# A macaron block on one core: the order of VectorE and ScalarE inside an attention step

## The chip, the cores and the metric

The kernel is written for one NeuronCore of a Trainium2 chip and runs on that core alone. The metric is device time in microseconds (us) of one execution, lower is better. TensorE, VectorE, ScalarE, GpSimd and SyncE are meant by these names; in rows of the profile they are PE (PEld for its weight loads), DVE, ACT, POOL and SP.

## What is computed

The input is x, 8 batches of 512 tokens of 128 values. Three layers follow, each on the layer-normed x and added to it: a mixture of experts (8 experts, top 2, hidden size 512) with weight one half, causal attention with 16 heads of 64, and the same mixture of experts again. The change touches the attention only:

```python
q = jnp.einsum('ahe,bce->bach', W_Q, x)
k = jnp.einsum('ahe,bce->bach', W_K, x)
v = jnp.einsum('ahe,bce->bach', W_V, x)
scores = jnp.einsum('bach,baCh->bacC', k, q)
masked = jnp.where(causal, scores, jnp.float32(-MASK_VAL))
attn = jax.nn.softmax(masked / np.float32(np.sqrt(D_HEAD)), axis=-1)
z = jnp.einsum('bacC,baCh->bach', attn, v)
out = jnp.einsum('aeh,bach->bce', W_O, z)
```

The rows of the scores belong to k, and the softmax runs over the tokens of q. Everything is fp32.

## The kernel before

Each engine has a program of its own, written out by hand, and semaphores join them. Nothing is scheduled by a planner: the order on an engine is the order of the calls in its function.

The attention is a loop of 64 steps (STEPS), eight for each batch; step i is one pair of heads of one batch, and its place in the batch is s. The 512 tokens of k are four tiles t of 128; causality makes tile t only (t + 1) x 128 columns wide, so a step has maxima and exponentials of 512, 384, 256 and 128 columns, two of each (heads h = 0, 1). A product of fp32 precision is made of high and low parts (split_matmul): ScalarE copies k and q from their banks rounded to k_hi and q_hi (take_k, take_q), VectorE subtracts these from the banks and gets k_lo and q_lo (split_k, split_q, "the low parts"), and the scores are three matmuls of them.

In a step i the engines do, in this order:

- TensorE: scores of tiles 3, 2, 1, 0 of step i; attend(i - 2), whose second half reads the late squares, which come by DMA; project_k and project_q of step i + 1 (they wait for the maxima of tile 2, whose banks they use); transposes(i - 1) of the early squares into the banks of tile 3; project_out(i - 2); project_v. The scores of step i + 1 wait for both low parts (qk_lo_ready) and for ScalarE's copies of the transposed squares (pt_act).
- VectorE: the maxima of tiles 3 (then the reciprocal of the last step's sums), 2, 1 and 0, which also add the mask and write the scores to SBUF; divide_by_sums(i - 2), which needs attend; turn_long, which turns the six late squares of each head by 32 x 32 blocks in two instructions; four pieces of side work; the low parts of step i + 1; up to seven more pieces of side work. Side work (go_on, finish) is layer norm and routing for other batches, spread over the steps by hand. In the fifth step of a batch (s = 4) it ends with split_for_attention, which makes xn_lo of the next batch.
- ScalarE: exps of tiles 3, 2 and 1; take_k and take_q of step i + 1; transposed(i - 1), two copies; exps of tile 0; take_v. At s = 4 and s = 5 (route_step) a further copy stands ahead of take_v.
- SyncE: store_sums and load_long of step i - 1, spread_sums, then store_long of step i: four stores of 192 KB of the turned squares to DRAM once turn_long has signalled, from where load_long fetches all of them in one DMA of 768 KB, back in the right place for attend. SyncE takes these one after another; load_long waits for the four stores (turned_stored) and for attend two steps back, whose late half reads the buffer it fills.

max_ready is what VectorE's maxima signal: S_USES = 3 times a step, after both heads of tile 3, after both of tile 2, after tiles 1 and 0.

## Time and profile before

| | before |
|---|---|
| time, median of 3 runs | 951.3 us (951.26 to 952.12) |
| the profiled execution: its own time, and its span | 942.84 us, 940.7 us |
| TensorE busy | 859.9 us, 91% of the span |
| VectorE busy | 812.2 us, 86% |
| ScalarE busy | 674.7 us, 72% |
| GpSimd busy | 279.9 us, 30% |
| mean granted clock of TensorE | 0.992 |

The attention steps lie between about 182 and 788 us of the span, the experts ahead of them and behind them. The profiled execution is one execution, and not one of the three that were timed. A row of the order in time has the start in us, the duration in us, the engine, the line of kernel.py, the operation, what it writes and reads and how many instructions it groups; in brackets how long the engine was idle just before it, and who ended that.

### The profile page before, as it was taken

The page shows a single profiled execution, that of the slowest core. Times are in us where ns is not written, and L with a number is a line of the kernel's source. Part 1 is how long each engine was busy: PE and PEld are TensorE (multiplying, and loading weights), DVE is VectorE, ACT ScalarE, POOL GpSimd, SP SyncE. Part 2 cuts the span into 40 slices and gives each one's busy share as a digit, 9 for nine tenths or more (in the row PEclk, how much of TensorE's full clock was granted, in tenths as well). Part 3 has the DMA queues.
Part 4 walks back from the last instruction along what each step waited for, and adds up shares of the span by engine and source line. Part 5 has one row for each costly group of instructions (what it writes and reads, how often), then busy time and mean ns, then how long its engine had stood idle before and what let it go on. Part 6 is the DMA issues. An engine that isn't in the chain of part 4 may idle for free.

```text
span 940.7 us, 24331 instructions
## 1 busy us (share of the span) xinstructions
PE 859.9 (91%) x7378; PEld 737.2 (78%) x7378; DVE 812.2 (86%) x3083; ACT 674.7 (72%) x1977; POOL 279.9 (30%) x328
## 2 busy tenths in 40 slices
PE   7999999978999998998998998999899888999994
PEld 6889998866777777776777776777687776999994
DVE  7878888789899899899999999989989996786666
ACT  3787667577777867785877786777686775787881
POOL 5777103241111021312321312310200102567551
PEclk9999999999999999999999999999999999999998
DMA  9677556177788688777687778676766785557657
GB/s 248 217 221 245 183 156 199 46 210 175 230 227 215 206 239 215 221 209 206 187 242 182 233 204 225 190 235 199 214 195 209 185 231 159 168 159 212 218 158 225
DMA packets 141296, 190.40 MB, mean 202 GB/s; under 512 B 35328, under 2 KB 108832, under 8 KB 141168
## 3 DMA queue, kind: packets, MB, share of 16 engines
q1 hardware_dynamic: 128256, 168.56, 61.1%
q0 software_dynamic: 8352, 18.17, 7.8%
q10 hardware_dynamic: 4560, 2.12, 0.8%
q8 instruction: 61, 1.00, 0.5%
q14 instruction: 67, 0.55, 0.2%
HBM read 114.04 MB, written 74.74 MB: 201 GB/s over the span
## 4 chain that ended last, share of the span: by engine, by line
PE 36%; DVE 25%; issue 5%; DMA 4%; SPq 2%; ACT 0%; POOL 0%; POOLq 0%; DVEq 0%; ACTq 0%
PE psum L2552 8%; PE psum L2502 7%; DVE arena L1975 6%; PE psum L2387 5%; DVE arena L1960 4%; PE psum L2338 3%; PE psum L2340 3%; PE psum L2339 3%; DVE arena L1990 3%; DVE q_lo L1947 2%; PE psum L2585 2%; PE psum L2541 2%; DVE k_lo L1951 1%; DMA turned_dram<-arena 1%; DVE bn L1243 1%
## 5 line engine op out<-in xcount | busy, mean ns | idle before, releaser
L1130 ACT ACTIVATE arena<-arena,neg_max 128x512 f32<-128x512 f32 (+3 forms) x512 | 281.5, 553 | 145.0 <-DVE neg_max L1960 142.7
L1960 DVE CUSTOM_DVE_ANT_0 arena<-psum,causal 128x512 f32<-128x512 f32 (+3 forms) x512 | 217.1, 480 | 29.0 <-PE psum L2502 28.5
L1074 ACT ACTIVATE arena<-psum,b_t 128x256 f32<-128x256 f32 (+1 forms) x336 | 120.8, 442 | 40.6 <-PE psum L2340 31.4
L876 POOL DMA_INDIRECT arena<-y_tiles,y_at x64 | 61.0, 953 | 277.6 <-PE psum L2502 194.3
L2387 PE MATMUL psum<-w_sb,arena 128*128 x1136 | 141.5, 276 | 0.2 <-ACT arena L1074 0.2
L2387 PEld LDWEIGHTS psum<-w_sb,arena 128*128 128x128 f32 x1136 | 134.9, 193 | 0.4 <-issue 0.4
L857 POOL DMA_INDIRECT x_slots<-xr,slot x64 | 61.9, 968 | 237.9 <-PE psum L2502 190.1
L2502 PE MATMUL psum<-q_hi,k_lo 64*128 64x512 f32 (+3 forms) x512 | 87.0, 332 | 42.0 <-DVE q_lo L1947 41.8
L1975 DVE STREAM_TRANSPOSE arena<-arena 128x768 f32<-128x768 f32 x126 | 115.7, 960 | 4.7 <-DMA turned_dram<-arena 2.8
L2502 PEld LDWEIGHTS psum<-q_hi,k_lo 64*128 64x128 f32 x512 | 49.0, 185 | 70.6 <-DVE q_lo L1947 65.0
L1130 ACT ACTIVATION_READ_ACCUMULATOR arena<-arena,neg_max 128x1 f32 x512 | 97.4, 190 | 0.0
L2552 PE MATMUL psum<-y_all,arena 128*64 128x128 f32 x1008 | 93.0, 327 | 2.3 <-DMA y_all<-turned_dram 2.3
L2502 PE MATMUL psum<-q_lo,k_hi 64*128 64x512 f32 (+3 forms) x512 | 84.1, 321 | 0.0
L2502 PE MATMUL psum<-q_hi,k_hi 64*128 64x512 f32 (+3 forms) x512 | 83.8, 319 | 0.0
L2552 PEld LDWEIGHTS psum<-y_all,arena 128*64 128x64 f32 x1008 | 66.2, 138 | 20.8 <-DMA y_all<-turned_dram 2.5
L885 POOL DMA_INDIRECT y_rows<-y_all,y_tok x69 | 67.4, 977 | 41.2 <-DVE y_all L1830 26.3
L1990 DVE TENSOR_TENSOR arena<-psum,arena 128x512 f32<-128x512 f32 x64 | 69.3, 1083 | 7.9 <-PE psum L2552 6.1
L857 POOL DMA_INDIRECT x_slots<-arena,slot x64 | 64.1, 1001 | 28.7 <-issue 16.2
L2552 PE MATMUL psum<-arena 128*64 128x128 f32 (+1 forms) x532 | 71.6, 392 | 0.2 <-ACT arena L1140 0.2
L1140 ACT ACTIVATE arena<-psum 128x512 f32<-128x512 f32 x129 | 68.6, 584 | 0.3 <-PE psum L2541 0.3
L2541 PE MATMUL psum<-ident,arena 128*128 128x128 f32 x524 | 67.8, 272 | 0.3 <-ACT arena L1140 0.3
L2585 PE MATMUL psum<-wo_t,arena 128*128 128x128 f32 x512 | 67.7, 275 | 0.2 <-DVE arena L1990 0.2
(361 smaller groups left out, 1989.9 us busy)
## 6 DMA issues: line engine op xcount, KB each, us to landing
turned_dram<-arena SPq DMA_DIRECT2D x252, 192.0 KB
y_all<-turned_dram SPq DMA_DIRECT2D x63, 768.0 KB, 5.2
arena<-inv_dram SPq DMA_DIRECT2D x128, 128.0 KB
w_raw<-in_L_ffn_W_dram SPq DMA_DIRECT2D x60, 256.0 KB
xg<-x_slots SPq DMA_DIRECT2D x43, 144.0 KB
arena<-in_L_ffn_W_dram SPq DMA_DIRECT2D x24, 256.0 KB
arena<-y_rows SPq DMA_DIRECT2D x16, 256.0 KB, 4.8
y_tiles<-y_all SPq DMA_DIRECT2D x27, 128.0 KB, 1.9
```

The lines of the kernel that those rows point to most:

```text
L857: pool.indirect_dma_start(out=x_slots[f][:, :], out_offset=bass.IndirectOffsetOnAxis(ap=slot[f][:, k, at_tile:at_tile + 1], axis=0), in_=r ...
L1074: ins = act.activation(h_t[side(f, n)][:, k, 0:rows], H_BANKS[side(f, n)][k // 2][:, k % 2 * rows:(k % 2 + 1) * rows], ACT.Relu, bias=b1_t ...
L1130: ins = act.activation(prob_tile(i, h, t), prob_tile(i, h, t), ACT.Exp, scale=-1.0, bias=neg_max[i % 2][:, h, t:t + 1], accum_out=row_sum[ ...
L1140: act.activation(four_turned(g), turned_bank(i, g), ACT.Copy).then_inc(pt_act, 1)
L1960: ins = dve.tensor_tensor_reduce(out=prob_tile(i, h, t), in0=score_tile(t, h), in1=causal[:, SEQ - (t + 1) * P:SEQ], scale=-1.0, scalar=-2 ...
L1975: ins = dve.transpose(long_block(h), long_probs(i, h).rearrange("p (n j s) -> p n j s", n=len(LATE_SQUARES), s=BLOCK))
L1990: dve.tensor_tensor(z_sb.rearrange("p (t q) -> p t q", t=QT), RING_C.rearrange("p (t q) -> p t q", t=QT), inv_bc[i % 2].rearrange("p q t - ...
L2387: ins = pe.matmul(Y_BANKS[side(f, n)][:, r * D:(r + 1) * D], h_t[side(f, n)][:, k, r * P:(r + 1) * P], w2_sb[:, bass.ds(e * (CHUNKS * D) + ...
L2502: ins = pe.matmul(score_tile(t, h), k[m, tile], q[m, 0:(t + 1) * P], start=(n == 0), stop=(n == 2))
L2541: ins = pe.transpose(turned_bank(i, g)[:, n * P:(n + 1) * P], probs[i % 2][h][:, col:col + P], ident[:, :])
L2552: return pe.matmul(RING_C[h * DH:(h + 1) * DH, tiles.start * P:tiles.stop * P], value(k, h), squares, start=start, stop=stop)
L2585: ins = pe.matmul(O_BANK[:, t * D:(t + 1) * D], z_sb[:, t * P:(t + 1) * P], wo_t[:, pair_cols(i)], start=(i % PAIRS == 0 and t == 0), stop ...
```

## The change

On ScalarE take_k and take_q of the next step go ahead of the exponentials of tile 1 (256 columns). On VectorE the low parts of the next step go ahead of turn_long and of the four pieces of side work. The maxima of tile 3 signal max_ready after each head, so that a step has four signals (MAXES) and no longer three, and exps waits for each head's own; all other waits on max_ready are renumbered for that.

```diff
-        S_USES, EXPS, PT_USES, PT_ACT, V_PAIRS = 3, 4, 2, 2, 4
+        S_USES, MAXES, EXPS, PT_USES, PT_ACT, V_PAIRS = 3, 4, 4, 2, 2, 4
...
             def exps(i, t):
-                act.wait_ge(max_ready, S_USES * i + min(QT - t, S_USES))
                 for h in range(2):
+                    act.wait_ge(max_ready, MAXES * i + (1 + h if t == QT - 1 else min(QT + 1 - t, MAXES)))
                     ins = act.activation(prob_tile(i, h, t), prob_tile(i, h, t), ACT.Exp, scale=-1.0,
...
                     exps(i, 3)
                     exps(i, 2)
-                    exps(i, 1)
                     if i + 1 < STEPS:
                         take_k(i + 1)
                         take_q(i + 1)
+                    exps(i, 1)
                     if i > 0:
                         transposed(i - 1)
...
-            def maxima(i, use, tiles):
+            def maxima(i, use, tiles, heads=range(2)):
...
                 for t in tiles:
-                    for h in range(2):
+                    for h in heads:
...
-                    maxima(i, 0, [3])
+                    maxima(i, 0, [3], [0])
+                    maxima(i, 0, [3], [1])
                     if i > 0:
                         invert(i - 1)
                     maxima(i, 1, [2])
                     maxima(i, 2, [1, 0])
                     if i > 1:
                         divide_by_sums(i - 2)
+                    if i + 1 < STEPS:
+                        split_k(i + 1)
+                        split_q(i + 1)
                     if i < STEPS - 1:
                         turn_long(i)
                     if i == STEPS - 2:
                         finish(work)
                     go_on(work, 4)
-                    if i + 1 < STEPS:
-                        split_k(i + 1)
-                        split_q(i + 1)
...
-                    pe.wait_ge(max_ready, S_USES * i + 2)
+                    pe.wait_ge(max_ready, MAXES * i + 3)
...
-                    pe.wait_ge(max_ready, S_USES * (i + 1))
+                    pe.wait_ge(max_ready, MAXES * (i + 1))
...
-                pe.wait_ge(max_ready, S_USES * STEPS)
+                pe.wait_ge(max_ready, MAXES * STEPS)
```

The rows below are the order of instructions on an engine, with the semaphores that each waits for. First ScalarE, one whole middle step before, from the exponentials of tile 3 to the copies of the transposed squares (L1130 is exps, L1120 take_k, L1116 take_q, L1140 transposed):

```order
L1130 ACTIVATE arena,row_sum<-arena,neg_max 128x512 [waits max_ready]
L1130 ACTIVATE arena,row_sum<-arena,neg_max 128x512
L1130 ACTIVATE arena,row_sum<-arena,neg_max 128x384 [waits max_ready]
L1130 ACTIVATE arena,row_sum<-arena,neg_max 128x384
L1130 ACTIVATE arena,row_sum<-arena,neg_max 128x256 [waits max_ready]
L1130 ACTIVATE arena,row_sum<-arena,neg_max 128x256
L1120 ACTIVATE k_hi<-psum 128x512 [waits qk_ps]
L1116 ACTIVATE q_hi<-psum 128x512 [waits s_ps,qk_ps]
L1140 ACTIVATE arena<-psum 128x512 [waits pt_ps,z_ps]
L1140 ACTIVATE arena<-psum 128x512 [waits pt_ps]
```

The same step on ScalarE with the change; x2 stands for the two heads, each with the wait:

```order
L1130 ACTIVATE arena,row_sum<-arena,neg_max 128x512 [waits max_ready] x2
L1130 ACTIVATE arena,row_sum<-arena,neg_max 128x384 [waits max_ready] x2
L1120 ACTIVATE k_hi<-psum 128x512 [waits qk_ps]
L1116 ACTIVATE q_hi<-psum 128x512 [waits s_ps,qk_ps]
L1130 ACTIVATE arena,row_sum<-arena,neg_max 128x256 [waits max_ready] x2
L1140 ACTIVATE arena<-psum 128x512 [waits pt_ps,z_ps]
L1140 ACTIVATE arena<-psum 128x512 [waits pt_ps]
L1130 ACTIVATE arena,row_sum<-arena,neg_max 128x128 [waits max_ready] x2
```

k_hi and q_hi now stand behind four exponentials and not behind six, and the two of 256 columns stand between them and the copies of the transposed squares.

Then VectorE in a middle step before, from the division to the next step's second longest maximum (L1990 is divide_by_sums, L1975 turn_long, L1951 and L1947 the low parts of k and q, L1960 the maxima, each followed by the read of its accumulator):

```order
L1990 TENSOR_TENSOR arena<-psum,arena 128x512 [waits o_ps,inv_loaded1,z_ps]
L1975 STREAM_TRANSPOSE arena<-arena 128x6x4x32 [waits turned_stored,exp_done]
L1975 STREAM_TRANSPOSE arena<-arena 128x6x4x32
L1951 TENSOR_TENSOR k_lo<-psum,k_hi 128x512 [waits k_hi_ready]
L1947 TENSOR_TENSOR q_lo<-psum,q_hi 128x512 [waits q_hi_ready]
L1960 ISA arena,neg_max<-psum,causal 128x512 [waits pt_ps,exp_done,s_ps]
L1960 ISA neg_max 128x1
L1960 ISA arena,neg_max<-psum,causal 128x512
L1960 ISA neg_max 128x1
```

The same place on VectorE with the change:

```order
L1990 TENSOR_TENSOR arena<-psum,arena 128x512 [waits o_ps,inv_loaded1,z_ps]
L1951 TENSOR_TENSOR k_lo<-psum,k_hi 128x512 [waits k_hi_ready]
L1947 TENSOR_TENSOR q_lo<-psum,q_hi 128x512 [waits q_hi_ready]
L1975 STREAM_TRANSPOSE arena<-arena 128x6x4x32 [waits turned_stored,exp_done]
L1975 STREAM_TRANSPOSE arena<-arena 128x6x4x32
L1960 ISA arena,neg_max<-psum,causal 128x512 [waits pt_ps,exp_done,s_ps]
L1960 ISA neg_max 128x1
L1960 ISA arena,neg_max<-psum,causal 128x512 [waits pt_ps,exp_done,s_ps]
L1960 ISA neg_max 128x1
```

The low parts moved ahead of both halves of the turning, and the second maximum of tile 3 has waits of its own; in this step there is no side work, which otherwise stands behind the turning.

## Rows read from the trace of the kernel before

**Rows 1.** The waits between 190 and 775 us: total us, times, longest us.

```profile
PE psum L2502 <- DVE q_lo L1947: 41.8, 40, 2.5
...
DVE arena L1960 <- PE psum L2502: 26.5, 30, 1.4
```

**Rows 2.** The order in time, one step without side work and the next one's start.

```profile
229.69 0.69 DVE L1960 CUSTOM_DVE_ANT_0 arena<-psum,causal 128x512 f32<-128x512 f32 x1 [0.28 <-PE psum L2502]
...
231.04 0.72 ACT L1130 ACTIVATE arena<-arena,neg_max 128x512 f32<-128x512 f32 x1 [1.65 <-DVE neg_max L1960]
...
231.67 1.47 PE L2552 MATMUL psum<-y_all,arena 128*64 128x128 f32 x16
...
233.07 0.50 PE L2338 MATMUL psum<-xn_hi,wk_lo 128*128 128x512 f32 x1
...
233.19 1.08 DVE L1990 TENSOR_TENSOR arena<-psum,arena 128x512 f32<-128x512 f32 x1
...
233.66 0.49 ACT L1130 ACTIVATE arena<-arena,neg_max 128x256 f32<-128x256 f32 x1
...
234.20 1.82 DVE L1975 STREAM_TRANSPOSE arena<-arena 128x768 f32<-128x768 f32 x2
...
234.33 0.39 PE L2340 MATMUL psum<-xn_hi,wq_hi 128*128 128x512 f32 x1
...
234.65 0.58 ACT L1120 ACTIVATE k_hi<-psum 128x512 fp32r<-128x512 f32 x1
...
235.60 1.06 ACT L1140 ACTIVATE arena<-psum 128x512 f32<-128x512 f32 x2
...
236.04 2.41 SPq L749 DMA_DIRECT2D turned_dram<-arena  x4
...
236.53 0.66 DVE L1947 TENSOR_TENSOR q_lo<-psum,q_hi 128x512 fp32r<-128x512 f32 x1
...
237.24 0.51 PE L2502 MATMUL psum<-q_hi,k_lo 64*128 64x512 f32 x2
...
238.26 0.69 DVE L1960 CUSTOM_DVE_ANT_0 arena<-psum,causal 128x512 f32<-128x512 f32 x1 [1.07 <-PE psum L2502]
...
238.59 0.28 PE L2502 MATMUL psum<-q_hi,k_lo 64*128 64x256 f32 x2
...
241.63 0.50 PE L2338 MATMUL psum<-xn_hi,wk_lo 128*128 128x512 f32 x1
...
242.31 0.34 SPq L758 DMA_DIRECT2D y_all<-turned_dram  x1
```

**Rows 3.** The order in time: a step's first maximum and its project_k.

```profile
501.66 0.67 DVE L1960 CUSTOM_DVE_ANT_0 arena<-psum,causal 128x512 f32<-128x512 f32 x1
...
504.03 0.51 PE L2338 MATMUL psum<-xn_hi,wk_lo 128*128 128x512 f32 x1
```

**Rows 4.** The order in time: first maxima of five steps, s = 4 to 7 and 0.

```profile
520.91 0.68 DVE L1960 CUSTOM_DVE_ANT_0 arena<-psum,causal 128x512 f32<-128x512 f32 x1
...
530.35 0.69 DVE L1960 CUSTOM_DVE_ANT_0 arena<-psum,causal 128x512 f32<-128x512 f32 x1 [0.46 <-PE psum L2502]
...
533.73 0.50 PE L2338 MATMUL psum<-xn_hi,wk_lo 128*128 128x512 f32 x1
...
539.22 0.69 DVE L1960 CUSTOM_DVE_ANT_0 arena<-psum,causal 128x512 f32<-128x512 f32 x1 [1.37 <-PE psum L2502]
...
548.54 0.69 DVE L1960 CUSTOM_DVE_ANT_0 arena<-psum,causal 128x512 f32<-128x512 f32 x1 [0.81 <-PE psum L2502]
...
557.78 0.69 DVE L1960 CUSTOM_DVE_ANT_0 arena<-psum,causal 128x512 f32<-128x512 f32 x1 [0.81 <-PE psum L2502]
...
566.49 0.69 DVE L1960 CUSTOM_DVE_ANT_0 arena<-psum,causal 128x512 f32<-128x512 f32 x1
```

**Rows 5.** The DMA issues between 190 and 775 us: count, KB each, median us to landing.

```profile
y_all<-turned_dram SPq DMA_DIRECT2D x62, 768.0 KB, 5.2
```

**Rows 6.** The order in time: the late half of the last but one attend.

```profile
784.67 0.33 PE L2552 MATMUL psum<-y_all,arena 128*64 128x128 f32 x2 [2.30 <-DMA y_all<-turned_dram]
```

## The prediction

> **What bounds the kernel now.** I read the waits of the attention stage first, since the diff touches nothing else. Two of them matter: TensorE waited 41.8 us in 40 places for the low part of q, and VectorE waited 26.5 us in 30 places for scores [rows 1]. So neither engine is the only bound: VectorE's order decides when TensorE may begin a step, and in other steps TensorE is late for VectorE. The second view is one step in order of time. I call T the start of a step's first maximum, K the start of project_k, S the first score matmul, and K − T the lag of TensorE. In the step from 229.69 [rows 2] the lag is 3.38. VectorE begins the division at T+3.50, the turning 1.01 later (234.20, 1.82 long), and the low parts end at 237.19. The next scores start at 237.24, behind project_v and not behind a gap: TensorE is full there, from K to the next S in 4.17 and from S to the next K in 4.39, 8.56 in all. VectorE's 1.07 of waiting in that step is TensorE's own length and no edit of VectorE's order removes it. The third view is the second half of a batch [rows 4]: periods 9.44, 8.87, 9.32, 9.24, with VectorE's waits of 0.46, 1.37, 0.81, 0.81 in them, and then one of 8.71 without. Less its waits VectorE needs 8.98, 7.50, 8.51, 8.43 and 8.71. The first half of a batch has no such wait; VectorE is full there, and the order of its work changes nothing in its sum.
>
> **The change part by part.** No instruction of work is added or removed. All times are reckoned from T or K by rows 2.
>
> The longest maxima signalled by head: ScalarE started at T+1.35, behind two maxima; it would start one earlier, half of that, at T+0.67. Its four long exponentials take 231.04 to 233.66, 2.62, so take_k could start at T+3.29 and take_q 0.48 later. But take_q needs project_q, whose last matmul ends at 234.72, K+1.65. Even with the lag of 2.37 where TensorE is not late [rows 3], that is T+4.02, later than T+3.77. The early signal is hidden by project_q: worth nothing by itself. The added waits find their value reached; their price is below a row's resolution, and I take nothing.
>
> k and q ahead of the short exponentials: k_hi, q_hi come out before two exponentials of 0.99 (233.66 to 234.65). What moves behind is transposed (1.06), and the next scores wait for it too, because it empties their banks. New chain: take_q at K+1.65+0.05 (0.05 is my estimate of one signal), half a copy pair 0.48, exponentials 0.99, transposed 1.06, a signal 0.05: K+4.28. TensorE is free at K+4.17. So where TensorE is full a step gets 0.1 longer, 8.67.
>
> The low parts ahead of the turning: q_lo cannot end before K+1.70+0.58 (copy, as k_hi's)+0.04+0.66 = K+2.98. VectorE itself could end it at T+3.50+1.01+1.17 = T+5.68 (1.17 is from the end of the turning to 237.19). With a lag over 2.70 VectorE therefore stalls by lag − 2.70, a wait that the old order covered with the turning. Where TensorE was idle the scores come sooner, and VectorE's wait for them shrinks.
>
> The turning itself comes later, and its four stores, the load of the transposed squares and the late half of attend with it, all on SP behind it. From K to the K two steps on: 2.98, turning 1.82, signal 0.03, four issues 2.41, landing 3.86 (238.45 to the load at 242.31), signal 0.05, load 5.2 [rows 5], signal 0.05, late part 1.40 (231.67 to 233.07): 17.80. Twice TensorE's 8.67 is 17.34, so this loop is the longer one in stretches where TensorE lags. The landing of the stores is the least certain term: 3.86 is one case in which the load waited for nothing else that I can see.
> A DMA's fixed part is given by the Trainium skill (DMA: Bandwidth & Descriptors, Anatomy of one DMA) as about 2.0 us plus bytes over 436 GB/s, fitted on GpSimd's path. By it a 192 KB store would land in 2.4 and the 768 KB load in 3.8, both estimates from that page, the loop would be 15.0, and the gain of a batch would be the 1.1 of the short-loop case below instead of 0.65. Rows 2 and 5 show 3.86 and 5.2, and I go by them.
>
> Ledger of one batch's second half, A = 0 [rows 4]. B: VectorE's 8.98 decides (scores come at about K+4.5, long before): B = 8.98. The scores of tile 1 wait for xn_lo, VectorE's last work before B; from them to K is 3.04 (238.59 to 241.63): K(B) = 8.98+0.05+3.04 = 12.07. From 533.73 to the next maximum at 539.22 is 5.49 (row transposes for the router in it): C = 17.56, before 18.31. K(C) = 12.07+5.49−1.02+4.39, and 0.18 for take_v, which ScalarE now does after more work: 21.11, lag 3.55, stall 0.85. D = 17.56+8.51+0.85 = 26.92. K(D) = max(21.11+8.67, 12.07+17.80) = 29.87, lag 2.95, stall 0.25. E = 26.92+8.43+0.25 = 35.60; before 36.87. K(E) = max(38.54, 21.11+17.80) = 38.91, lag 3.31, so step E stalls 0.61 and ends at 44.92. Then K = 38.91+8.67 or 29.87+17.80 = 47.67, lag 2.75, stall 0.05, and the long steps behind it absorb the rest. Gain of a batch: 36.87 − 35.60 − 0.61 = 0.65.
>
> Sum: seven such batches, 4.6. The first step has no division: its turning waits for the long exponentials (T+1.35+2.62, and 0.1 for the last), then 1.82, the low parts 1.17, scores and 1.02 to the next maximum make 8.1, and TensorE's longest wait, 2.5 [rows 1], is such a one. Now the low parts end at K+2.98 = T+5.35 and the turning at T+7.17: 1.0 less. In the second, as long, scores at K+4.28 = T+6.65 allow a period of 7.67: 0.5 less. The first batch's full TensorE steps lose 0.1 to 0.2 each: −0.4 (estimate). The end loses: in the last step TensorE waited 2.30 for the last load [rows 6], and no later step absorbs it; the turning is later by the low parts' 1.17, so that wait grows by as much, and the experts behind it start later. Sum: 4.6+1.5−0.4−1.2 = 4.5. The profiled execution had 942.84 (span 940.7), 0.9% under the median of 951.3; it becomes 938.3, and the median 946.8.
>
> **The rivals.** First, VectorE becomes the only bound and all its 26.5 us of waiting [rows 1] go: 951.3 − 26.5 = 924.8. For it: its pair may come 1.82 sooner than now. Against it: in rows 2 TensorE has no gap, and its own 8.56 is longer than VectorE's 7.50. A milder form, the loop through DMA shorter than 17.3: K(D) = 29.78, K(E) = 38.45, stalls 0.16 and about 0.3 in place of 0.25 and 0.61, a gain of 1.1 a batch and 943.7.
>
> Second, slower: the load of the turned squares takes over. One mechanism: the turned squares land late, attend stalls in its late half, the lag rises, and each step's low parts stall VectorE by it. If stores and load together take 0.8 more than 9.06 (the load is a median, and DMA engines are well used), the loop is 18.60: K(D) = 30.67, stall 1.05, E = 36.40, stall 0.61, and the step after it (K = 30.67+18.60 = 49.27, lag 3.55) another 0.85. Against 36.87 that is a loss of 0.14 and 0.85, 1.0 a batch, 7.0 in all; the start gives 1.5 back, the first batch and the end take 1.6: 7.1 lost, 958.4. It decides from about 0.4 more, where by the same sum a batch gains nothing.
>
> Third, no change: the new chain of q, short exponentials and transposed holds the scores as long as the old one of the low parts did. For it: 0.1 lies between K+4.28 and TensorE's 4.17, and a further 0.2 of signals per step would eat the 0.65 of a batch. Then start and end cancel and the time is 951.
>
> **How the numbers follow.** What a measurement of this kernel tells from no change is about 0.2%, 1.9 us. Chances: the forecast with its milder form, gain 2 to 10: 0.58. VectorE alone: 0.08. No change: 0.19. Slower: 0.15. So faster 0.66, same 0.19, slower 0.15. The range reaches from 938 (half way to what full cover of VectorE's waits would give) to 953 (the loop 0.5 longer); the forecast's own range is 941 to 949.
>
> **What the changed profile would show.** Right: TensorE's waits for q_lo fall from 41.8 to under 15, and some turn into waits for ScalarE's copy of the transposed squares; new waits of VectorE for k_hi or q_hi, together 5 to 15 us, in steps with a lag; periods of 8.6 to 8.8 where there is no side work, near 9.0, 8.6, 9.3, 8.7 in the stretch of rows 4; SP's load issued behind the stores' landing in most steps instead of behind attend; the wait of 2.30 at the end near 3.5. ScalarE starting 0.6 sooner with nothing else moved by it. Wrong: no waits of VectorE for k_hi or q_hi (then the lag is smaller than I hold, and the gain larger), or waits of TensorE for the loaded squares in most steps (the second rival).

## The result and the profile after

The change made the kernel slower: 967.44 us (median of 4 runs, 963.9 to 972.9) against 951.28 us for the kernel before (median of 4 runs, 950.99 to 952.12), a ratio of 1.017 with a 95% interval of 1.012 to 1.023. The forecast was 946.8 us, with a range of 938 to 953. In a second group of runs the change gave 1.0156 [1.0125, 1.0186].

The page of the changed kernel, its span and busy times (the profiled execution took 963.90 us):

```profile
span 962.2 us, 24393 instructions
PE 873.6 (91%) x7378; PEld 744.1 (77%) x7378; DVE 821.0 (85%) x3083; ACT 691.8 (72%) x1977; POOL 280.7 (29%) x328
```

Its span is 21.5 us longer than before's 940.7. I cut both traces at the first maximum of each step. The first lies at 182.4 us (182.8 before), the last at 793.4 (775.1): 18.7 of the 21.5 us lie between them, and 3.2 behind them. The length of a step by its place in the batch, in us, is the median over six batches, the first and the last left out. Versions from the experiments stand beside it for later: in e4_join GpSimd's addition is held back, e6_turn_first has the turning ahead of the low parts, and the last two have the low parts early in three steps of a batch only:

| | s=0 | 1 | 2 | 3 | 4 | 5 | 6 | 7 | sum | last batch, 7 steps |
|---|---|---|---|---|---|---|---|---|---|---|
| before | 8.73 | 10.27 | 9.67 | 9.58 | 9.44 | 8.87 | 9.32 | 9.24 | 75.12 | 67.18 |
| the change | 9.41 | 10.65 | 9.84 | 9.70 | 9.85 | 8.88 | 9.65 | 9.14 | 77.12 | 71.77 |
| with the join held (e4_join) | 9.06 | 10.80 | 9.83 | 9.71 | 8.89 | 8.87 | 9.63 | 9.10 | 75.88 | 71.71 |
| turning first (e6_turn_first) | 8.77 | 10.26 | 9.97 | 9.72 | 8.90 | 8.88 | 9.63 | 8.75 | 74.86 | 69.04 |
| three steps (e12_three_steps) | 8.81 | 10.92 | 9.67 | 9.65 | 8.88 | 8.87 | 9.32 | 8.92 | 75.05 | 67.14 |
| three steps, two places (e13_two_buffers) | 8.77 | 10.26 | 9.68 | 9.64 | 8.88 | 8.88 | 9.32 | 8.56 | 73.98 | 67.71 |

Only s = 7 gained with the change. The waits between 190 and 790 us (total us, times, longest us), which answer to [rows 1] (those end at 775, but up to 790 their two sums are the same):

```profile
PE psum L2339 <- DVE neg_max L1960: 17.6, 20, 1.6
DVE k_lo L1951 <- ACT k_hi L1120: 14.8, 35, 0.7
DVE arena L1960 <- PE psum L2503: 12.7, 17, 3.6
PE psum L2553 <- DMA y_all<-turned_dram: 9.9, 13, 2.4
PE psum L2503 <- ACT arena L1140: 8.7, 30, 1.2
PE psum L2503 <- DVE xn_lo L1844: 7.9, 6, 1.7
```

TensorE's 41.8 us of waiting for q_lo are gone. In their place it waits for VectorE's maxima before project_k, for ScalarE's copies, for xn_lo and for the loaded squares: 44.1 us in these four rows. VectorE waits half as long for scores, but 14.8 us for k_hi. The wait moved; it did not go away.

SyncE's waits in the same stretch, first before and then with the change:

```profile
SPq L499 <- PE psum L2552: 84.9, 61, 3.0
...
SPq L758 <- DMA turned_dram<-arena: 15.8, 17, 2.0
```

```profile
SPq L758 <- DMA turned_dram<-arena: 128.1, 56, 3.9
...
SPq L499 <- PE psum L2553: 44.2, 40, 3.3
```

L499 is the wait for attend, L758 the load of the turned squares behind the stores. The stores, which had landed by the time that the load could go in most steps, now are what it waits for in 56.

Four places carry most of the loss. First, s = 4. The order in time with the change, where side work (L1292, four normalisations) is the last but one thing that VectorE does in the step:

```profile
536.67 2.02 DVE L1292 TENSOR_SCALAR xr<-xs,mean,rstd 128x128 f32<-128x128 f32 x4
...
537.32 1.28 POOL L865 TENSOR_TENSOR xs<-xs,arena 128x512 f32<-128x512 f32 x1 [7.29 <-PE psum L2503]
...
538.61 0.68 DVE L1844 TENSOR_TENSOR xn_lo<-psum,xn_hi 128x512 fp32r<-128x512 f32 x1
...
539.21 0.67 DVE L1960 CUSTOM_DVE_ANT_0 arena<-psum,causal 128x512 f32<-128x512 f32 x1
```

The same work before:

```profile
527.01 1.08 DVE L1292 TENSOR_SCALAR xr<-xs,mean,rstd 128x128 f32<-128x128 f32 x4
...
530.40 1.28 POOL L865 TENSOR_TENSOR xs<-xs,arena 128x512 f32<-128x512 f32 x1 [7.45 <-PE psum L2502]
```

The same four instructions take 2.02 in place of 1.08. GpSimd's join (L865, an addition of the experts' results) is let go by the step's first scores. Before, these came when VectorE was at its maxima, and the addition ran beside them at no cost. Now the scores come while VectorE normalises, and the addition falls into that. VectorE's step is full, so it gets 0.94 longer: 9.85, where 8.9 would have been a gain of 0.55.

Second, TensorE's clock. Windows of two successive steps: length, then the busy time of PE, PEld, DVE, ACT and POOL with their instructions, the granted clock, the DMA share and GB/s:

```profile
606.79:616.65 9.86, 7.55 (x62) 5.90 (x57) 9.86 (x29) 7.52 (x22) 2.49 (x3) 1.00 0.77 203
616.65:627.11 10.46, 10.24 (x75) 8.04 (x77) 7.63 (x24) 7.23 (x22) 2.69 (x3) 0.84 0.55 164
```

In the step of the collision TensorE was busy 7.55 of 9.86 us; in the next its mean granted clock is 0.84, so that a part of it ran at 1.2 GHz and the rest at 2.4, and the step took 10.46 instead of 8.88. This run has that once. The second run of the change has it three times (10.51, 10.47, 10.53, each at 0.84), so behind four of the eight collisions in all.

Third, s = 0. With the change:

```profile
490.41 0.69 DVE L1960 CUSTOM_DVE_ANT_0 arena<-psum,causal 128x512 f32<-128x512 f32 x1
...
493.56 0.50 PE L2339 MATMUL psum<-xn_hi,wk_lo 128*128 128x512 f32 x1
...
493.76 1.05 DVE L1990 TENSOR_TENSOR arena<-psum,arena 128x512 f32<-128x512 f32 x1
...
495.19 0.69 DVE L1951 TENSOR_TENSOR k_lo<-psum,k_hi 128x512 fp32r<-128x512 f32 x1 [0.38 <-ACT k_hi L1120]
```

VectorE is done with the division 4.40 after the step's start, and k_hi comes at 4.78. The lag K − T is 3.15 here. Nothing else of VectorE's stands between, so it idles 0.38 in a step in which it had no idle time before. The step goes from 8.73 to 9.02.

Fourth, three single places: step 2, a step in the last batch, and the last load.

```profile
205.19 1.09 DVE L1990 TENSOR_TENSOR arena<-psum,arena 128x512 f32<-128x512 f32 x1 [4.55 <-DMA arena<-inv_dram]
...
770.09 0.63 PE L2220 MATMUL psum<-ident,xr 128*128 128x128 f32 x4 [2.46 <-DVE xr L1292]
...
773.54 0.69 DVE L1960 CUSTOM_DVE_ANT_0 arena<-psum,causal 128x512 f32<-128x512 f32 x1 [3.60 <-PE psum L2503]
...
804.04 2.10 PE L2553 MATMUL psum<-y_all,arena 128*64 128x128 f32 x16 [3.73 <-DMA y_all<-turned_dram]
```

Step 2 takes 13.53 (10.09 before): the spread sums land late. In the last batch TensorE transposes xr in the very step in which VectorE makes it; that side work now stands behind the low parts and the turning, TensorE waits 2.46 in front of the next scores, and VectorE 3.60 for these. The step takes 11.71 (9.37 before), at a granted clock of 0.88; in the second run of the change, where the clock stood at 1.00, the same step took 10.55. The last load is waited for 3.73 where it was 2.30 [rows 6].

### The profile page after: what moved, and what is told of

The parts are those of the page before. It is cut to its first block, busy times and chain, and to the rows that moved or that the text cites. A ratio compares the mean times of both kernels' runs of the same rounds, so it can differ in the third digit from the quotient of the medians.

```text
span 962.2 us, 24393 instructions
## 1 busy us (share of the span) xinstructions
PE 873.6 (91%) x7378; PEld 744.1 (77%) x7378; DVE 821.0 (85%) x3083; ACT 691.8 (72%) x1977; POOL 280.7 (29%) x328
## 4 chain that ended last, share of the span: by engine, by line
PE 35%; DVE 26%; DMA 17%; issue 8%; ACT 5%; SPq 5%; POOL 4%; DVEq 0%; POOLq 0%; ACTq 0%
PE psum L2388 8%; DMA turned_dram<-arena 7%; DVE arena L1975 7%; PE psum L2553 7%; DVE arena L1960 5%; PE psum L2339 4%; PE psum L2503 4%; PE psum L2341 3%; POOL x_slots L857 3%; PE psum L2340 3%; DMA y_all<-turned_dram 3%; SPq L749 2%; DVE arena L1990 2%; ACT arena L1130 2%; DVE k_lo L1951 2%
## 5 line engine op out<-in xcount | busy, mean ns | idle before, releaser
L1130 ACT ACTIVATE arena<-arena,neg_max 128x512 f32<-128x512 f32 (+3 forms) x512 | 282.4, 555 | 114.5 <-DVE neg_max L1960 107.3
L1960 DVE CUSTOM_DVE_ANT_0 arena<-psum,causal 128x512 f32<-128x512 f32 (+3 forms) x512 | 216.9, 479 | 14.7 <-PE psum L2503 14.7
L1975 DVE STREAM_TRANSPOSE arena<-arena 128x768 f32<-128x768 f32 x126 | 115.2, 953 | 3.4 <-DMA turned_dram<-arena 2.7
L2503 PE MATMUL psum<-q_hi,k_lo 64*128 64x512 f32 (+3 forms) x512 | 92.2, 337 | 20.2 <-ACT arena L1140 8.7
L1130 ACT ACTIVATION_READ_ACCUMULATOR arena<-arena,neg_max 128x1 f32 x512 | 97.4, 190 | 0.0
L2503 PEld LDWEIGHTS psum<-q_hi,k_lo 64*128 64x128 f32 x512 | 53.0, 186 | 51.0 <-issue 43.7
L2503 PE MATMUL psum<-q_lo,k_hi 64*128 64x512 f32 (+3 forms) x512 | 88.4, 322 | 0.0
L2503 PE MATMUL psum<-q_hi,k_hi 64*128 64x512 f32 (+3 forms) x512 | 87.8, 321 | 0.0
L1990 DVE TENSOR_TENSOR arena<-psum,arena 128x512 f32<-128x512 f32 x64 | 69.2, 1081 | 18.8 <-PE psum L2553 12.1
L1140 ACT ACTIVATE arena<-psum 128x512 f32<-128x512 f32 x129 | 69.0, 586 | 0.3 <-PE psum L2542 0.3
```

The source lines that it names most:

```text
L1130: ins = act.activation(prob_tile(i, h, t), prob_tile(i, h, t), ACT.Exp, scale=-1.0, bias=neg_max[i % 2][:, h, t:t + 1], accum_out=row_sum[ ...
L1140: act.activation(four_turned(g), turned_bank(i, g), ACT.Copy).then_inc(pt_act, 1)
L1960: ins = dve.tensor_tensor_reduce(out=prob_tile(i, h, t), in0=score_tile(t, h), in1=causal[:, SEQ - (t + 1) * P:SEQ], scale=-1.0, scalar=-2 ...
L1975: ins = dve.transpose(long_block(h), long_probs(i, h).rearrange("p (n j s) -> p n j s", n=len(LATE_SQUARES), s=BLOCK))
L1990: dve.tensor_tensor(z_sb.rearrange("p (t q) -> p t q", t=QT), RING_C.rearrange("p (t q) -> p t q", t=QT), inv_bc[i % 2].rearrange("p q t - ...
L2503: ins = pe.matmul(score_tile(t, h), k[m, tile], q[m, 0:(t + 1) * P], start=(n == 0), stop=(n == 2))
```

## The experiments

Ratios are to the kernel before on the same chip, with a 95% interval in brackets. Line numbers in versions lie up to eight above those of before.

**Parts of the change by themselves.** e1_heads has only the signals by head:

```diff
-        S_USES, EXPS, PT_USES, PT_ACT, V_PAIRS = 3, 4, 2, 2, 4
+        S_USES, MAXES, EXPS, PT_USES, PT_ACT, V_PAIRS = 3, 4, 4, 2, 2, 4
```

> The longest maxima signalled by head, alone; both orders as before. Theory L (the turned squares land late, because the turning moved behind the low parts): the turning stays where it was, so 951, within 1.5 of before. Theory A (ScalarE's new order holds the scores): also 951. A gain above 2 us would say that my reading was wrong in which ScalarE's start is hidden by project_q; with the copies of k and q behind six exponentials, the start is not hidden by it, so up to 0.6 a step could come through in the steps in which the low parts wait for ScalarE, which I saw in none.

Measured: 0.9998 [0.9967, 1.0028]. No gain of the early signal can be seen, as forecast.

e2_act has, besides, ScalarE's new order; VectorE's is the old one.

> Signals by head and ScalarE's new order; VectorE's order as before. Theory L: the turning is early again, so the loads wait for attend and not for the stores; 949 to 953, SyncE's load waits for the stores in under 25 steps (56 with the change), no wait of VectorE for k_hi. Theory A: the loss stays, 960 or more, with TensorE waiting for ScalarE's copy of the transposed squares before the scores.

Measured: 1.0004 [0.9965, 1.0043], as theory L had it: SyncE's load waited for the stores in 16 steps. A batch is 75.40 long, and s = 6 is 9.65 where it was 9.32. Of the change's steps that one is ScalarE's doing.

e3_dve is the kernel before with VectorE's new order alone:

```diff
+                    if i + 1 < STEPS:
+                        split_k(i + 1)
+                        split_q(i + 1)
                     if i < STEPS - 1:
                         turn_long(i)
```

> VectorE's new order alone; ScalarE as before, signals as before. Theory L: the turning is late and later still, because the low parts now wait for a k_hi that comes behind six exponentials (about T+5.5 where VectorE is there at T+4.5): 1 us of wait a step, so slower than with the whole change, 968 to 990. Theory A: 951 to 955, since ScalarE's order is the old one.

Measured: 1.0597 [1.0522, 1.0673], a batch of 85.25. The wait is the 1 us a step that was expected, but the loss is larger than the 968 to 990 us (up to 1.041) that were reckoned from it. The wait for k_hi (190 to 790 us):

```profile
DVE k_lo L1951 <- ACT k_hi L1120: 56.1, 56, 2.2
```

So VectorE's order can only be had with ScalarE's, and with both 14.8 of these 56.1 us are left.

**The join.** e4_join is the change with one wait added to GpSimd, so that the addition falls beside the maxima again:

```diff
                 if s == JOIN_STEP + early // 2 and b + 2 < BATCH:
+                    pool.wait_ge(max_ready, MAXES * i + 1)
```

> The whole change, and GpSimd's join of the next batch waits for VectorE's first maximum of its step too, where it waited for the first scores alone. With the change its 1.28 us additions begin at 537.3 inside VectorE's four normalisations of the fifth step, which take 2.02 instead of 1.08. Theory J (these two collide): that step's period falls from 9.85 to 8.9 in the batches that show it, 4 to 6 us in all: about 962. Theory L for the rest: the other steps keep their periods (9.65 in the seventh, 9.4 in the first). If J is wrong the step stays 9.85.

Measured: 1.0108 [1.0070, 1.0147]. s = 4 went from 9.85 to 8.89 and none of the middle steps s = 5 had a lower clock. Against the two results of the change the ratio is 0.006 or 0.005 lower; the intervals nearly touch, so that the size rests on the trace more than on the times. It shows the first cause, and that it is not the main one.

**The landing.** e5_other_squares is e4_join with the load of the squares no longer behind its own step's stores. Attend's late half is computed from the squares of the step before.

```diff
-                sp.wait_ge(turned_stored, stored_long(i + 1))
+                sp.wait_ge(turned_stored, stored_long(max(i, 1)))
...
-                sp.dma_start(late_t, turned_dram[i % 2]).then_inc(late_loaded, 16)
+                sp.dma_start(late_t, turned_dram[max(i - 1, 0) % 3]).then_inc(late_loaded, 16)
```

> As e4_join (the change, join behind the first maximum), but the load of the late squares fetches those of the step before from one of three DRAM buffers, whose stores landed long ago, so it waits for attend and not for the landing of its own step's stores; the late part of the attention is then computed from the wrong step's squares. The turning, the stores, the bytes and all orders stay. Theory L (the landing of late stores is what the change pays): the medians of the first, second steps of a batch fall from 9.06 and 10.80 to 8.75 and 10.3, the batch from 75.9 to 74.5 or less, and the ratio to before is 0.985 to 0.998. If the stalls come from elsewhere (ScalarE's chain, side work whose result TensorE needs in the same step), the batch stays above 75.5 and the ratio above 1.003.

Measured: 1.0124 [1.0065, 1.0183], a batch of 75.53 in place of 75.88. SyncE's waits for the stores fell from 116.4 to 27.9 us (190 to 790 us) and the kernel was no faster. VectorE's wait for k_hi stayed, at 12.9 us in 30 places for 14.4 in 32. The landing ahead of the load, on which the second rival stood, is not the main cause.

**The turning first.** e6_turn_first is the change with the order turning, low parts, side work; e7_turn_first_join has the join held as well.

```diff
-                    if i + 1 < STEPS:
-                        split_k(i + 1)
-                        split_q(i + 1)
                     if i < STEPS - 1:
                         turn_long(i)
+                    if i + 1 < STEPS:
+                        split_k(i + 1)
+                        split_q(i + 1)
```

> The change, but the low parts stand behind the turning and ahead of the four pieces of side work (in between the two orders). Theory L: the turning is where it was, so loads wait for attend again (under 25 waits for the stores), nothing of the 1.6% stays; steps with side work give the scores up to 0.9 sooner, so the fifth step falls from 9.44 to about 9.0, the seventh and eighth by 0.3: a batch of 74 to 75, ratio 0.990 to 0.999. If the position of the side work is what costs (it is as late as in the change), the ratio stays above 1.005.

> e6_turn_first with GpSimd's join behind the first maximum as in e4_join. If join collides with the normalisations here too, the fifth step is 0.9 shorter than in e6_turn_first in the batches that show it, ratio 0.004 lower; if not, the two are equal.

Measured: 1.0007 [0.9982, 1.0031] and 0.9996 [0.9971, 1.0021]. The whole loss is gone, and the gain that theory L expected (0.990 to 0.999) did not come. From e4_join to e7_turn_first_join only the place of the turning changes, and the ratio goes from 1.0108 to 0.9996: that the low parts stand ahead of the turning is the main cause. k_hi is there when the turning ends, s = 0 and 1 are back at 8.77 and 10.26, and with the scores later again the join misses the normalisations by itself. What s = 4 and s = 7 gain (0.54 and 0.49) goes in s = 2, 3 and 6 (0.30, 0.14, 0.31) and in the last batch (1.86).

**The sums.** e8_sums_first is e4_join with SyncE's spread_sums ahead of load_long, to mend step 2.

> e4_join with the load of the spread sums ahead of the load of the late squares on SyncE. The single wait of VectorE's division for the spread sums (4.55 in the third step with the change) goes, since the sums no longer stand behind a load that waits for landing; the load of the squares waits then for the sums' round trip of 2.3 to 3 us, less than it waits for the stores where that is 3 us or more, more elsewhere. I expect 0 to 4 us less than e4_join; if the round trip is the longer wait in most steps, 5 us more.

Measured: 1.1026 [1.0959, 1.1093], where at most 5 us more than e4_join were expected. The waits behind 190 us, of SyncE and then of TensorE:

```profile
SPq L738 <- DMA inv_dram<-inv_sum: 231.4, 64, 6.2
```

```profile
PE psum L2554 <- DMA y_all<-turned_dram: 75.9, 45, 5.6
```

SyncE takes its DMAs in order. The sums' round trip through DRAM, which the load used to cover, now holds the load of the squares back in every step.

**The ends.** e9_after_again is the change, e10_ends_old is e4_join with VectorE's old order in the first three steps and the last batch (`ahead = 2 < i < STEPS - PAIRS`), e11_ends_old_other_squares has the load of e5 besides (its late half is computed from the wrong step's squares too).

> The change itself again, beside the three other versions of this group. Every theory expects its ratio of before, 1.012 to 1.022; it is the mark against which the others are read.

> The change with GpSimd's join held until the step's first longest maximum, and with VectorE's old order (turning, side work, low parts) in the first three steps and in the whole last batch. Theory of the ends: the part of the loss that is left after the join's repair (1.0108) comes almost all from single places, where work that another engine waits for in the same step stands behind the low parts: step 2 (13.4 long) goes back to about 10, the last batch from 70 to about 68, the wait for the last load from 3.7 to 2.3, about 9 us together: ratio 0.999 to 1.003. Rival, the late stores and loads cost something in every step: then the middle batches stay at 75.9 and their loss is what remains, and the ratio stays over 1.005.

> The version before it (VectorE's old order at both ends, join repaired) in which, besides, the load of the turned squares no longer waits for the stores of its own step but fetches the step before's; attend's late half is therefore computed from the wrong squares. Theory of the ends: the landing costs a batch 0.3 to 0.5 us, so 2 to 4 us are gained, ratio 0.003 lower than without it. If the loop through the DMA were the bound of the middle steps, the batch would fall from 75.9 to 74 or under and the ratio by 0.01 or more.

Measured: 1.0156 [1.0125, 1.0186], 1.0036 [1.0013, 1.0060] and 1.0101 [1.0072, 1.0130]. With the old order at the ends step 2 is 10.38 and the last batch 68.64, where e4_join had 10.43 and 71.71 and the change 13.53 and 71.77. Step 2 goes with the two steps ahead of it: 13.53, 13.33 and 13.38 in the change, its second run and e5_other_squares, where these take 7.08 or 7.09 and 7.72 to 7.74, but 10.43 in e4_join, where they take 7.57 and 8.98 (the second at a granted clock of 0.81). The last batch lost 2.7 to 2.9 by the order (69.85 in e14_change_two_buffers and 70.04 in the second run of the change, where the clock stayed at 1.00, for 67.18 before) and the rest by the clock. The batches between stay at 76.02, 0.9 longer than before: each theory holds in part. The third version was expected to be faster than the second and was slower. VectorE's wait at the turning in it:

```profile
DVE arena L1976 <- DMA turned_dram<-arena: 8.0, 9, 1.4
```

It was 3.7 in e10_ends_old. turn_long writes the place that the stores of the step before read, so it waits until these have landed; with the load going out earlier beside them they landed later. It also had more steps at a lower clock (0.82 to 0.93 in seven).

**Three steps only.** e12_three_steps is the kernel before with the join held and with the low parts between turning and side work at s = 4, 6 and 7; ScalarE and the signals are old.

```diff
+                    ahead = s in (4, 6, 7) and 2 < i < STEPS - PAIRS
                     if i < STEPS - 1:
                         turn_long(i)
+                    if ahead:
+                        split_k(i + 1)
+                        split_q(i + 1)
```

> The kernel before, with the join held until the first longest maximum, and with the low parts between the turning and the side work in three steps of a batch only (s = 4, 6, 7, from the fourth step on, not in the last batch); ScalarE's order and the signals are those of before. Theory: what the change gains lies in these steps alone, s = 4 at 8.9 instead of 9.44 and s = 7 at 8.75 instead of 9.24, and s = 6 keeps its 9.32 because ScalarE's order is old: a batch of 74.1 to 74.4 instead of 75.1, ratio 0.992 to 0.996. Rival: the gain of these steps is given back in s = 0 to 2, where VectorE is full, and the ratio is 0.999 to 1.001, as with the turning ahead everywhere.

Measured: 0.9975 [0.9954, 0.9995], less than expected. s = 4 has its 8.88, but s = 1 is 10.92 (10.27 before). The order in time in such an s = 1, first SyncE, then VectorE's turning:

```profile
417.01 1.46 SPq L749 DMA_DIRECT2D turned_dram<-arena  x2
...
423.26 0.34 SPq L758 DMA_DIRECT2D y_all<-turned_dram  x1
```

```profile
423.34 1.84 DVE L1976 STREAM_TRANSPOSE arena<-arena 128x768 f32<-128x768 f32 x2 [1.50 <-DMA turned_dram<-arena]
```

The last two stores are issued by 418.47 and let go of the turning's place some 4.8 later. VectorE waits 1.50 for it, and with it the low parts, the side work and TensorE. In this version such waits sum to 10.5 us in 15 places (2.8 in 3 before).

**A second place for the turned squares.** e13_two_buffers is e12_three_steps with two places in SBUF by turns, so that the turning waits for the stores two steps back. e14_change_two_buffers is e4_join with it, e15_before_two_buffers the kernel before with it.

```diff
-        turned = probs_t[:, 8 * P:20 * P]
+        turned = [y_all[:, 0:12 * P], probs_t[:, 8 * P:20 * P]]
...
-                wait(dve, turned_stored, stored_long(i))
+                wait(dve, turned_stored, stored_long(i - 1))
```

> The version with the low parts ahead of the side work in three steps of a batch (ratio 0.9975), with a second place in SBUF for the turned squares, so that the turning waits for the stores of the step before the last one only, not of the last. Theory of the stores: VectorE's 10.5 us of waiting for stores at the turning (15 places there) go, s = 1 comes back from 10.9 to about 10.3, the batch from 75.05 to 74.3, ratio 0.990 to 0.994. Rival, the load behind the same stores takes over: TensorE waits for the loaded squares instead, by as much, and the ratio stays at 0.996 to 0.999.

> The change with the join held until the first longest maximum, and with the second place for the turned squares. Theory: its turning waits for stores only 1 to 3 us in all, so the turning's own wait is not what the change loses; the batch falls by 0.1 to 0.3 from 75.9 and the ratio stays within 0.003 of 1.0108. Rival, the stores' landing ahead of the turning is the missing part: batch at 75.1 or under, ratio 1.003 or under.

> The kernel before with the second place for the turned squares and nothing else. It waited 2.8 us in 3 places for stores at the turning. Every theory expects 0.997 to 1.000; it is the mark for the two others.

Measured: 0.9927 [0.9904, 0.9949], 1.0105 [1.0074, 1.0135] and 0.9952 [0.9929, 0.9974]. The three-step version now has 10.26 at s = 1 and 8.56 at s = 7, a batch of 73.98, and beats the kernel before and the change; of its gain the second place alone gives more than half. The change gains nothing by it: its batch is 75.81 (75.88 without), and the turning's wait is not what it loses.

The second place alone gave more than any theory expected (0.997 to 1.000). Its batch is no shorter in the median (75.07 for 75.12). What it takes away are single waits of the turning for the stores, 2.8 us in 3 places before and 6.2 in 8 in e1_heads, which has both old orders; that these are the 0.5% is argued from their size and was not tested. Nor do the medians and the times agree on how the two edits join: by the batch the three steps gain 0.07 without the second place and 1.09 with it, by the ratio 0.0025 either way.

## Why the prediction was wrong

**What held.** The head signal is worth nothing (0.9998). The chain K+4.28 behind ScalarE's new order made TensorE wait for transposed: 8.7 us in 30 places, 0.29 each where 0.1 was reckoned. VectorE's waits for k_hi are 14.8 us, at the upper end of 5 to 15, and TensorE's for q_lo are gone. The first two steps took 7.08 and 7.74 where 7.1 and 7.67 were reckoned. SyncE's load stands behind the landing in 56 steps, and the last wait is 3.73 for a forecast of 3.5. The mechanisms were there. The balance was wrong: a batch was to take 0.65 less and took 2.0 more. With the join held it took 0.76 more (e4_join); of the 1.4 between that and the forecast, 0.6 lie in the five steps of the ledger and 0.8 in s = 1 to 3 behind it. The steps of the prediction that failed are these.

**The tally** of the 18.7 us between the first and the last step: the first batch lost 2.2 (1.5 gained in two steps, 3.4 lost in step 2), the last 4.6, and the six between 12.0: 3.8 by the join in s = 4, 1.6 by the clock behind it, and 6.6 as what is left of the losses in s = 0 to 3 and 6 when the gains of s = 7, and of s = 4 but for the join, are taken off.

**"VectorE's 8.98 decides: B = 8.98."** With the join held it is 8.89, so the sum of VectorE's work was right. It left out that a third engine is released by the same scores. The prediction asked what is late next, but not what would be early. The join took 0.96 in each of four batches (9.85 to 8.89, e4_join), about 3.8 of the 18.7 us, and one lower clock behind it a further 1.6. The experiment's ratio, 0.005 to 0.006 lower, is some 5 to 6 us.

**"K(D) = max(21.11+8.67, ...)": the ledger behind B.** With the join held the five steps took 8.89, 8.87, 9.63, 9.10 and 9.06, where the ledger has 8.98, 8.58, 9.36, 8.68 and 9.32. In all that is 45.55 for 44.92, with 45.60 before: 0.05 gained where the ledger had 0.65. Two of its terms for TensorE were too small. The rows of s = 5 and 6 with the join held, L1961 being the maxima, L2504 the scores and L2340 project_k:

```profile
564.01 0.69 DVE L1961 CUSTOM_DVE_ANT_0 arena<-psum,causal 128x512 f32<-128x512 f32 x1
...
564.25 0.38 PE L2504 MATMUL psum<-q_hi,k_lo 64*128 64x256 f32 x2 [0.77 <-DVE xn_lo L1845]
...
567.40 0.50 PE L2340 MATMUL psum<-xn_hi,wk_lo 128*128 128x512 f32 x1
...
571.88 0.49 PE L2504 MATMUL psum<-q_hi,k_lo 64*128 64x512 f32 x2
...
572.88 0.69 DVE L1961 CUSTOM_DVE_ANT_0 arena<-psum,causal 128x512 f32<-128x512 f32 x1 [0.73 <-PE psum L2504]
...
576.56 0.50 PE L2340 MATMUL psum<-xn_hi,wk_lo 128*128 128x512 f32 x1
...
581.50 0.50 PE L2504 MATMUL psum<-q_hi,k_lo 64*128 64x512 f32 x2
```

In s = 5 the scores of tile 1 start 0.24 behind the maximum (0.05 in the sum) and reach project_k 3.15 later (3.04), so that the lag is 3.39 and not 3.09, as long as before; the step stays at 8.87, as in every version of the table. In s = 6 TensorE takes 4.94 from project_k to the next scores. The 8.67 has 4.28 for that, read in a step without side work, but here TensorE also has the router's matmuls (L2226, 0.96), and the trace of the kernel before shows 4.93:

```profile
542.60 0.50 PE L2338 MATMUL psum<-xn_hi,wk_lo 128*128 128x512 f32 x1
...
545.85 0.96 PE L2226 MATMUL psum<-wr_sb,xt 128*128 128x8 f32 x8
...
547.53 0.50 PE L2502 MATMUL psum<-q_hi,k_lo 64*128 64x512 f32 x2
```

So TensorE and not VectorE sets the length of s = 6, and with ScalarE's new order the lag there is 3.68 (3.38 before): 9.63, which e2_act shows by itself (9.65). In s = 7 VectorE waits 0.43 for k_hi in each of the six batches, where 0.25 was reckoned, and in two of them also for attend at the division.

**"The long steps behind it absorb the rest."** This is the reasoning that failed. A step in which VectorE is full absorbs a delay of TensorE, not an idle time of VectorE's own. The stall of s = 0 was in the ledger, and with 0.61 at a lag of 3.31 set too high (0.38 at 3.15 in the row shown; a load or a store that is late as well makes the step up to 9.5 long). But s = 1 was given a lag of 2.75 and a stall of 0.05, and s = 2 and s = 3 nothing, and with the join held they took 0.53, 0.16 and 0.13 more than before. In s = 1 VectorE's waits at the division, the low parts and the turning come to 0.3 to 1.35 in four of six batches; with the change the step takes up to 11.6. That the turning ahead of the low parts takes these stalls away, and the losses of s = 0, 1 and 7 with them, is shown by e6_turn_first.

**"The order of its work changes nothing in its sum"** in the first half of a batch. s = 2 and s = 3 got 0.16 and 0.13 longer without a wait. The low parts had stood between two side instructions of which the second reads the first's result; now these follow each other. In the changed trace such dependent pieces of 0.12 to 0.21 start 0.15 to 0.21 apart, and independent ones of that size 0.08 to 0.11, so that the dependence costs where nothing fills it. This was read from the order and the rows only; no experiment took it apart. The two steps s = 1 without a wait took 0.11 and 0.13 more than before as well.

**The single places.** The sum had 1.5 gained at the start, 0.4 lost in the first batch and 1.2 at the end. The start did gain 1.5, and step 2 lost 3.4 behind it. In e4_join step 2 took only 10.4, but two steps that together took 1.7 longer stood ahead of it; no run has the full 1.5 and a short step 2 behind it. The last batch lost 4.6 and was not in the sum at all: side work moved behind the low parts is itself waited for by TensorE in that batch. Without a fall of the clock it is 2.7 to 2.9. From the last first maximum on, 3.2 were lost, where the load's wait (1.4) is what the prediction had. In the 20 us behind that maximum the granted clock was 0.91 with the change and 1.00 before; what of the rest is due to that was not measured.

**The second rival**, slower through late landing, came out on the right side and for the most part for another reason. From the last store's issue to the load's it was 4.3 us on average (2.9 to 5.8) for the reckoned 3.86, about its point of decision. But taking that wait away gave a batch only 0.35 (e5_other_squares), and in e11_ends_old_other_squares it gave nothing. What stays open is how the irregular part of s = 0 and 1 splits between late loads, late stores and the k_hi stall: the three come together, and removing one let another show.

## What to carry to other kernels

When work is moved so that a signal comes earlier, list everything that waits for that signal, on every engine, and look at what each will then run beside; an early helper can cost more than the early signal brings. Put a consumer ahead of other work only where its input is ready at that moment: on an engine that is full, such a wait of 0.4 us is lost, and the filler that used to cover it (here the turning) was free. Check first and last rounds by themselves, and before reordering around a buffer that a DMA still reads, ask whether a second buffer is to be had: here it was worth 0.5% with no reordering and 0.7% with a small one. And where a step's length is reckoned from an engine's own work, read that work in the step itself: the 0.65 us that the ledger lacked for TensorE in s = 6 stood in the trace of the kernel before.

## What the runs showed of the hardware

An addition of GpSimd on 128x512 floats in SBUF, 1.28 us long, stretched four normalisations of VectorE on 128x128 floats from 1.08 to 2.02 us; one of the four took 1.29, the shortest 0.30, and the addition kept its 1.28:

```profile
537.40 1.29 DVE L1292 TENSOR_SCALAR xr<-xs,mean,rstd 128x128 f32<-128x128 f32 x1
```

With the addition held back (e4_join) the four take 1.08 again. The Trainium skill (SBUF — State Buffer, Who interferes with whom) says that VectorE's tensor-scalar operations can enter a mode in which they need the port pair shared with GpSimd, and that the loser blocks for the whole instruction of the other. The one instruction of 1.29 beside an addition of 1.28 agrees with that. Beside the maxima, which read PSUM and SBUF, the same addition changed nothing: the one at 530.35 in [rows 4], with the addition from 530.40, took 0.69, and so did the one at 539.22 without it.

TensorE's granted clock fell in single steps. In mid-batch the mean was 0.84 or 0.85 in steps that took 1.5 to 1.7 us longer than the same step at 1.00 (10.46 to 10.53 for 8.87, and 11.04 for 9.58). It came behind four of the eight collision steps, in which TensorE was busy about 7.5 of 9.86 us. But the kernel before has one such step as well (11.04 us at 0.85), without a collision, behind a step in which TensorE was busy 7.79 of 9.69 us; the same step of the next batch, busy 7.79 of 9.67, had none behind it. What brings the fall is therefore not shown, and it cannot be put down to a single step in advance.

The chips differed more than the versions: in five groups of runs the kernel before took 945.09, 948.76, 951.28, 995.31 and 1002.65 us. In the traces of the two slow groups the first maximum came at 205 to 212 us instead of 181 to 184, and 189 to 194 us lay behind the last one instead of 166 to 173, while a batch took the same 75.07 (e15_before_two_buffers, 75.12 before). So the difference lies for the most part in the experts ahead of the attention and behind it. Ratios are each from one chip; step lengths were compared across chips.
